# A four-layer transformer on one core: each batch normalised and turned in the last stage of the batch before it, and the running sum loaded by a second transfer

## What is computed

```python
xn = _layernorm(x, axis=-1)
x = x + attn(xn) + ffn(xn)
```

## Time and profile before

| | |
|---|---|
| median of 3 runs | 4661.18 us (4642.65 to 4664.65) |
| the profiled execution's own time | 4653.22 us |
| its span, first to last instruction | 4651.5 us |
| mean granted TensorE clock | 0.885 of full speed |
| TensorE busy | 3614.1 us, 78% |
| VectorE busy | 2547.1 us, 55% |
| ScalarE busy | 1866.7 us, 40% |
| Pool busy | 707.9 us, 15% |
| device memory read, written | 108.57 MB, 50.33 MB |

### The profile page before, as it was taken

The page is one execution under the profiler, slowest core; times in us unless marked ns, Lnnn a source line. Parts: engine busy times, 40 slices in busy tenths (PEclk is TensorE's granted clock), DMA queues, the critical chain, the costliest instruction groups (busy, mean ns, idle before and its releaser), DMA issues. The chain is left out here.

```text
span 4651.5 us, 61071 instructions
## 1 busy us (share of the span) xinstructions
PE 3614.1 (78%) x22440; PEld 2158.7 (46%) x22440; DVE 2547.1 (55%) x5300; ACT 1866.7 (40%) x2789; POOL 707.9 (15%) x862
## 2 busy tenths in 40 slices
PE   5776768667658888687873977877897897897898
PEld 3433334143333635335362655655662672572572
DVE  5656657466664453545436353452664664764764
ACT  3372552624445363543612333433216306306306
POOL 3101120121110000100001222322220220230230
PEclk8898889878879989899986978988899899899899
DMA  4403214124310000000001000001000000000000
GB/s 162 128 11 109 87 51 124 32 69 123 99 44 1 10 10 5 15 1 10 10 30 41 5 14 18 5 14 57 10 1 11 10 1 10 10 1 10 10 1 10
DMA packets 130451, 159.40 MB, mean 34 GB/s; under 512 B 16128, under 2 KB 106752, under 8 KB 130048
## 3 DMA queue, kind: packets, MB, share of 16 engines
q1 hardware_dynamic: 121664, 135.20, 9.1%
q0 software_dynamic: 6144, 16.79, 1.1%
q10 hardware_dynamic: 2320, 3.28, 0.2%
HBM read 108.57 MB, written 50.33 MB: 34 GB/s over the span
## 5 line engine op out<-in xcount | busy, mean ns | idle before, releaser
L601 DVE TENSOR_REDUCE arena<-ps 128x2 f32<-128x1024 f32 (+3 forms) x768 | 698.6, 952 | 153.8 <-PE ps L569 95.2
L790 ACT ACTIVATE arena<-ps 128x1024 f32<-128x1024 f32 (+3 forms) x768 | 572.6, 813 | 127.5 <-PE ps L703 79.1
L871 DVE TENSOR_TENSOR arena<-arena,tri 128x256 f32<-128x256 f32 x512 | 211.3, 424 | 353.0 <-ACT arena L790 322.7
L703 PE MATMUL ps<-arena 64*128 64x512 f16 (+3 forms) x1536 | 255.8, 349 | 147.7 <-ACT arena L790 87.0
L720 PE MATMUL ps<-arena 128*17 128x512 f32 (+3 forms) x3072 | 342.5, 519 | 6.7 <-DVE arena L871 4.0
L790 ACT ACTIVATE attention<-ps 128x1024 f32<-128x1024 f32 (+3 forms) x384 | 287.9, 809 | 130.2 <-PE ps L703 130.2
L2253 ACT ACTIVATE arena<-ps 128x256 f32<-128x256 f32 x192 | 63.6, 381 | 614.7 <-PE ps L2195 576.7
L703 PEld LDWEIGHTS ps<-arena 64*128 64x128 f16 x1536 | 70.3, 94 | 497.9 <-ACT arena L790 400.6
L720 PE MATMUL ps<-attention 128*33 128x512 f32 (+3 forms) x1536 | 288.3, 498 | 0.0
L569 PE MATMUL ps<-arena 64*128 64x512 f16 (+3 forms) x1536 | 235.1, 332 | 50.3 <-DVE arena L601 29.8
L367 PE MATMUL ps<-arena 128*128 128x512 f32 (+1 forms) x768 | 271.5, 502 | 0.0
(11 more groups left out here) (310 smaller groups left out, 6653.7 us busy)
## 6 DMA issues: line engine op xcount, KB each, us to landing
arena<-w_experts SPq DMA_DIRECT2D x128, 256.0 KB
x_next<-sums SPq DMA_DIRECT2D x16, 1024.0 KB
arena<-slots_x SPq DMA_DIRECT2D x32, 512.0 KB, 4.6
slots_y<-arena SPq DMA_DIRECT2D x32, 512.0 KB, 4.4
sums<-arena SPq DMA_DIRECT2D x24, 512.0 KB, 2.8
making<-basis SPq DMA_DIRECT2D x16, 768.0 KB, 5.5
slots_x<-arena SPq DMA_DIRECT2D x1, 4096.0 KB, 24.6
out<-arena SPq DMA_DIRECT2D x8, 512.0 KB, 2.8
```

The lines of the kernel that those rows point to most:

```text
L601: dve.reduce_max(a.mp[:, 2 * j:2 * j + 2, qt, c], out[:, :, 0:w], AX.X).then_inc(self.pair_out, 1)
L703: last = pe.matmul(m.ps[:, 4 + 2 * (v % 2) + odd, q0:CH], a.k[half, pair, kt * P:(kt + 1) * P], a.q[half, pair, c * CH + q0:(c + 1) * CH], ...
L790: act.activation(a.p[:, v % ring, :, q0:CH], m.ps[:, b:b + 2, q0:CH], ACT.Exp, scale=HD ** -0.5).then_inc(exped, 1)
L871: dve.tensor_tensor(diag, diag, keep, ALU.min).then_inc(masked, 1)
```

## The change

The normalisation of a batch leaves its first stage. It is done in the last stage of the batch before it, among that stage's other work (new class `NextNormalisation`); the very first one gets a stage of its own ahead of the first loop. In detail:

- `m.x` is normalised directly, without a copy into `m.acc`. `m.xn` and `m.xn_t` become tensors of their own, which live across stages and layers; the arena shrinks to make room.
- `m.acc` is filled by a second transfer from device memory. `begin_batch`, in the batch's first stage, waits on SyncE for the stores of the batch before, then issues that transfer and the one for the next batch's `m.x`. The first operation that adds to `m.acc` waits for it (`m.acc_in`).
- In `attention` with a store (layers 0 and 3): VectorE takes one tile's statistics in each of blocks 0 to 7, aggregates in block 8, takes the reciprocal in block 11 and applies to two tiles in each of blocks 11 to 14; ScalarE takes the root ahead of exponential 20; TensorE turns two tiles at the end of each of blocks 12 to 15 (banks 2 and 3), and VectorE (not ScalarE) copies them out in blocks 13 to 16.
- In `gated_ffn`: statistics in units 2 to 9, aggregation in unit 10, root in unit 11, reciprocal in unit 12, applications in units 12 and 13; TensorE turns two pairs of tiles after unit 14 and two after unit 15, and VectorE copies all four after its last split. The pairs of PSUM banks for the units go from three to two; the options for an RMS norm, unused here, are gone.
- In `mixing_layer`: statistics and aggregation after `join(10)`, root after the square of n = 4, applications after `join(12)` and `join(13)`, turns and copies beside down products 2 to 5, whose PSUM ring goes from four banks to two. The second normalisation starts the stage.
- In layer 3 the output bias is added by Pool at the start of `lora_experts`.

```diff
+def begin_batch(sp, m, src, batch):
     for chunk_stored in m.stored:
+        sp.wait_ge(chunk_stored, 16)
         sp.sem_clear(chunk_stored)
+    sp.dma_start(m.acc[:, :, :], tiles_of(src)[:, bass.ds(batch * NT, NT), :]).then_inc(m.acc_in, 16)
     sp.dma_start(m.x[:, :, :], tiles_of(src)[:, bass.ds(batch * NT + NT, NT), :]).then_inc(m.x_in, 16)
...
+class NextNormalisation:
...
+    def scalar_root(self, act):
+        act.wait_ge(self.spread, NT + 1)
+        act.activation(self.std, self.veps, ACT.Sqrt).then_inc(self.rooted, 1)
...
+    def tensor_turn(self, pe, i, bank):
+        pe.wait_ge(self.normed, 2 * (i + 1))
+        if i >= 2:
+            pe.wait_ge(self.kept, i - 1)
+        for k in range(KD):
+            for j in range(2):
+                last = pe.transpose(self.m.ps[:, bank, (2 * k + j) * P:(2 * k + j + 1) * P],
+                                    self.m.xn[:, 2 * i + j, k * P:(k + 1) * P], self.m.ident[:, :])
+        last.then_inc(self.turned, 1)
+
+    def vector_keep(self, dve, i, bank):
+        dve.wait_ge(self.turned, i + 1)
+        dve.tensor_copy(self.m.xn_t[:, :, 2 * i * P:2 * (i + 1) * P],
+                        self.m.ps[:, bank, :].rearrange("p (k n) -> p k n", k=KD)).then_inc(self.kept, 1)
...
 def attention_operands(...)
-            norm.tensor(pe)
             pe.wait_ge(*weights)
...
-            norm.vector(dve, weights)
...
-            norm.scalar(act)
...
 def attention(...)
+                if ahead is not None and 0 <= block - NEXT_TURN < NT // 2:
+                    ahead.tensor_turn(pe, block - NEXT_TURN, 2 + (block - NEXT_TURN) % 2)
                 if block in finishing:
...
+                if ahead is not None and v == 2 * NEXT_ROOT:
+                    ahead.scalar_root(act)
...
+                if ahead is not None:
+                    if block < NT:
+                        ahead.vector_stats(dve, block)
+                    if block == NT:
+                        ahead.vector_spread(dve)
+                    if block == NEXT_TURN - 1:
+                        ahead.vector_scale(dve)
+                    if 0 <= block - NEXT_TURN + 1 < NT // 2:
+                        for t in range(2 * (block - NEXT_TURN + 1), 2 * (block - NEXT_TURN + 2)):
+                            ahead.vector_apply(dve, t)
+                    if 0 <= block - NEXT_TURN - 1 < NT // 2:
+                        ahead.vector_keep(dve, block - NEXT_TURN - 1, 2 + (block - NEXT_TURN - 1) % 2)
...
 def gated_ffn(...)
-                if n >= 3:
-                    pe.wait_ge(gated, n - 2)
+                if n >= 2:
+                    pe.wait_ge(gated, n - 1)
...
+                if n >= units - 2:
+                    for i in range(2 * (n - units + 2), 2 * (n - units + 3)):
+                        ahead.tensor_turn(pe, i, 4 + i % 2)
             down(NC - 1)
...
             split(units - 1)
+            for i in range(NT // 2):
+                ahead.vector_keep(dve, i, 4 + i % 2)
             add(NC - 1)
...
 def mixing_layer(...)
-            first.tensor(pe)
             ffn_up(0)
             ffn_up(1)
-            pe.wait_ge(first.stored, NT // 2)
             second.tensor(pe)
...
 def lora_experts(...)
+            pool.wait_ge(m.acc_in, 16)
+            pool.tensor_tensor(m.acc[:, :, :], m.acc[:, :, :], out_bias[:, :].unsqueeze(1).broadcast_to([P, NT, D]),
+                               ALU.add).then_inc(biased, 1)
...
+            first_normalisation(nc, m)
             with nc.Fori(0, B) as b:
```

More of the change, by code:

```diff
@@ L306, in attention_operands, with norm_places @@
-def attention_operands(nc, m, a, out_bias, wqkv, bias, table, rms, heads, vd, weights, routed=None, w_router=None):
+            for k in range(KD):
+                last = act.activation(self.dst_t[:, k, cols], pair[:, k, :], ACT.Identity,
+                                      bias=self.scale_b[:, k:k + 1], scale=self.scale_w[:, k:k + 1])
+            last.then_inc(self.stored, 1)
+def norm_places(m, place):
+    small = m.norm[:, place, :]
+    return (small[:, 0:2 * NT].rearrange("p (t c) -> p t c", c=2), small[:, 2 * NT:8 * NT].rearrange("p (t c) -> p t c", c=6),
+            *(small[:, i * NT:(i + 1) * NT] for i in range(8, 11)))
@@ new lines, in first_normalisation, with _ @@
+def first_normalisation(nc, m):
+    with stage(nc, *NextNormalisation.SEMAPHORES) as (block, *sems):
+        ahead = NextNormalisation(m, sems)
+        @block.vector
+        def _(dve):
+            for t in range(NT):
+                ahead.vector_stats(dve, t)
+            ahead.vector_spread(dve)
+            ahead.vector_scale(dve)
+            for t in range(NT):
+                ahead.vector_apply(dve, t)
+            for i in range(NT // 2):
+                ahead.vector_keep(dve, i, 4 + i % 2)
+        @block.scalar
+        def _(act):
+            ahead.scalar_root(act)
+        @block.tensor
+        def _(pe):
+            for i in range(NT // 2):
+                ahead.tensor_turn(pe, i, 4 + i % 2)
+        @block.sync
+        def _(sp):
+            ahead.sync_end(sp)
@@ L310, in attention_operands @@
+def attention_operands(nc, m, a, wqkv, bias, table, rms, heads, vd, weights, src, batch, after=None, routed=None,
+                       w_router=None):
     gh = 2 * NM
@@ L627, in sync_rows, with attention @@
         self.sync_end(sp)
-def attention(nc, m, a, maps, width, wout, out_scale, batch, fetch=None, store=None, routed=None):
+def attention(nc, m, a, maps, width, wout, out_scale, batch, store=None, routed=None):
     groups, pairs = NM // maps, maps // 2
@@ L729, in turn @@
                     pe.wait_ge(evac, groups * (c + 1))
+                    if c == 0 and half == 0 and ahead is not None:
+                        pe.wait_ge(ahead.kept, NT // 2)
                 if c == 0 and u >= 1:
@@ L928, in gated_memory, with gated_ffn @@
     return f
-def gated_ffn(nc, m, f, wg, wu, wd, rms, batch, store):
+def gated_ffn(nc, m, f, wg, wu, wd, batch, store):
     ni = F1 // P
     units = NC * ni
-    with stage(nc, "x_high", "x_low", "upped", "silued", "gated", "high", "low", "square_even", "square_odd", "summed",
-               "downed", "added", "steps", "sumsq", "ms_in", "rms_done", pool=rms) as \
-            (block, x_high, x_low, upped, silued, gated, high, low, square_even, square_odd, summed,
-             downed, added, steps, sumsq, ms_in, rms_done):
-        ms, root, inv = (m.small[:, i * NT:(i + 1) * NT] for i in range(3))
-        def sums(c):
-            return m.ps[:, 0 if c == NC - 1 else 7, 0:TC]
-        def adds(n):
-            return (ni - 1) * (n // ni) + n % ni
-        products = [(0, 0), (0, 1), (1, 0)][:1 + len(wg)]
+    with stage(nc, "x_high", "x_low", "upped", "silued", "gated", "high", "low", "downed", "added",
+               *NextNormalisation.SEMAPHORES) as \
+            (block, x_high, x_low, upped, silued, gated, high, low, downed, added, *next_sems):
+        ahead = NextNormalisation(m, next_sems)
+        products = [(0, 0), (0, 1), (1, 0)]
         @block.sync
         def _(sp):
+            sp.sem_clear(m.acc_in)
+            ahead.sync_end(sp)
             store_sums(sp, m, store, batch, added)
```

309 lines of the change are left out of this document (145 added, 164 removed).

## The result

Six executions of the changed kernel took 4614.77 to 4635.23 us, median 4621.53; six of the kernel before, beside them, had a median of 4653.01. The ratio is 0.9938, with an interval of 0.9921 to 0.9955: 31.5 us faster, 0.7%. The forecast was 73.6 us of gain. The direction and the wide range (4540 to 4635) held; the forecast's own range (4560 to 4615) did not, and less than half of the gain came.

A forecast was written before the change was run, and what follows sets the result against it. No engine is always busy; the normalisation at batch seams was taken to lie wholly on the path. Gain 174.7 less costs 101.1 gives 73.6 us: 4579.6 from the profiled 4653.2, median forecast 4587 (-1.6%), range 4540 to 4635.

The forecast's parts named there:

- The head: Seam between two batches: idle stretch while the normalisation runs before the first projection, wholly on the path; removing it gains 174.7 us.
- After the change TensorE waits there for the weights alone: Seams of layers 0, 1 and 3: first projection 0.1 to 0.3 us into each stage.
- The clock: Start of attention_operands: the 1.2 GHz stretch falls on projections, 2.3 us lost in 11 batches, 25 (bounds 0 and 40).
- What it slows is VectorE: with Pool busy an operation of 0.42 becomes 0.77: Layer 3's lora_experts: two or three VectorE operations slowed by Pool's bias, 0.7 us a batch, 2.8 (bounds 0 and 20).
- The root: Attention of layers 0 and 3: ScalarE's square root with two table loads costs 2.8 us a stage, 22.4 over eight.
- The turns with their copies: Attention of layers 0 and 3, blocks 12 to 15: waits on VectorE cost 3.5 us a stage, 28.0 in all.
- The drain rival: Attention of layers 0 and 3: each table switch holds exponentials another 1.4 us, 22 more, giving 4609; chance 0.07.
- the lock of three engines: Attention: each turn costs a block of VectorE, 11.6 us instead of 3.5, giving 4652, no change; chance 0.13.
- The pause in front of the last down: Layer 1's gated_ffn: TensorE's pause of 2.22 us grows by 1.9, to about 4 with turns in it.
- Layer 2: mixing_layer: 9.5 us gained four times, 38.0, less 9.6 for transposes and waits on copies at the end.
- The first stage: First normalisation as its own stage ahead of the loop: 11.6 us against the 9.9 it replaces, +1.7.
- Other: Catch-all rival, such as a head staying in part because Pool's memsets or another wait end last; chance 0.08.

## Why the prediction was right in kind and too large

- *The head is gone, but a part of it was never the head's.* The step that failed is "After the change TensorE waits there for the weights alone", with 12.7 to 13.4 us booked as removable at nine seams. Some 2.8 of these were the branch's and no work of the head, and another 1.28 a table load that is gone with the loop; after the change 3.7 to 4.1 us stand before the first projection at each of the nine seams, where 0.1 to 0.3 was forecast, and 0.11 with the loops written out. The timeline gave the hint: layer 1's first head was 9.9 us, with no branch ahead of it. I put the difference of 3 down to the store; it was this. From the memset to VectorE's first take layer 3's seam took 16.42 us and now takes 9.27. The seams of batches 2 to 4 fell short by 3.0 us each in layer 0, 2.1 in layer 1 and 2.9 in layer 3, 23.9 in all; the two first batches of layers 1 and 3, where no branch stands, came out at 8.3 and 7.7 where 7.6 was forecast.
- *The clock.* Right in its place: the projections' first 24 took 10.82 us against 8.79, 2.0 more where 2.3 was taken, and the first four microseconds stood at 0.50 where they had been at 0.77. With the loop written out the 24 took 9.67, so a part of this loss too came with the branch. The window in the kernel after:

```profile
4273.60:4277.60 4.00, 3.94 (x5) 1.85 (x6) 0.00 (x0) 0.94 (x1) 0.00 (x0) 0.50 1.02 309
```

- *Pool's bias.* The second step that failed, and as large: "What it slows is VectorE: with Pool busy an operation of 0.42 becomes 0.77". 2.8 taken, 25.1 measured, outside even the bound of 20. I priced a slowdown of VectorE by the nearest rows, 0.42 to 0.77, for some three operations, and 1.25 us for each quarter of Pool's work. The size of Pool's work was right (5.01). Wrong was the kind: VectorE was held for the whole rest of it (3.57 to 4.98 instead of 0.69), and TensorE behind it. The Trainium skill has it (SBUF — State Buffer, Who interferes with whom): a VectorE instruction with two SBUF inputs contends with a GpSimd instruction that reads SBUF, and the port pair that they share is an exclusive lock. The rows agree. The bias moved off Pool gave 4.3 to 5.0 us a batch in one place and 5.7 to 6.2 in the other.
- *Attention.* 6.3 forecast, 7.3 measured. The root: 2.8 taken, 2.8 to 3.6 shown. The turns with their copies: 3.5 taken, 2.3 shown. Statistics and applications: taken as fitting in VectorE's gaps apart from the turns; 1.4 to 2.2 are left for them. So the sum came close in part because the turns were taken too dear and the rest too cheap. The drain rival is out (the run without root), the lock of three engines too.
- *gated_ffn.* 2.9 taken, 3.5 on the mean. The pause in front of the last down is as worked out.
- *Layer 2.* 28.4 forecast, 34.4 measured. The first product came 4.9 us after the opening, 4.4 was taken; so its costs at the end were well under the 9.6 booked. No run parts these. This miss was luck: it offset 6 us of the others.
- *The first stage.* +1.7 taken, +5.2 measured: the stage takes 14.7 us, and attention_operands behind it became 9.5 shorter. The copies stand behind all applications, and TensorE's turns 2 and 3 behind the copies.
- *Chances.* Faster had 0.81, and it was. The case that came had no name among the rivals; a head that stays in part stood under *Other*, with 0.08.

The misses sum to 55.2 us in the profiles, 24 of them at the seams, 22 from the bias and 8 in attention; 13.7 of them are that this one execution lay above its median.

## What to carry to other kernels

Before a head is booked as removable, compare it with a seam of the same work that has no branch ahead (a loop's first pass): what differs is not the head's work and may stay, as it did here. Here writing the loops out was worth more, 37 us, than the change, 31. Work handed to an idle Pool is not free because Pool is idle: look whether VectorE reads two SBUF inputs in that time, and look for a pause of VectorE itself first; 2.3 us in such a pause did what 5 us of Pool beside it could not. And a chain of small operations costs its length in a queue where others wait behind it (2.2 us here); spread over blocks, together with earlier statistics, it cost little.

## What the runs showed of the hardware

- A loop's branch back held TensorE 3.3 to 3.8 us a time in layers 0, 1 and 3 of the kernel after (rows of its queue) and 0.2 in layer 2. In layer 3 ScalarE began 2.8 to 3.3 us after the memset, with no record of it on its own branch (45 ns).
- A 128x2048 addition took 4.5 to 5.0 us on Pool and 2.29 on VectorE. On Pool it stretched a VectorE operation with two SBUF inputs from 0.69 us to 3.57 to 4.98, ending each time 0.55 us behind Pool; those with one input in PSUM kept their 0.68 us.
- A switch to the root's table and back within exponentials took 2.82 us from the first load to the next exponential, with no additional drain.
- The same program took 2.4% less on another chip (4540 against 4653), about 100 of the 113 us in layer 0's experts and attention; it was one execution there, and why is not shown.
